# A decoder block on one core: two sets of one-hot and weight tiles, with other tensor work between the banks of the outer products

## What is computed

```python
xn = batch_norm(inputs)                        # over all 1792 tokens
q = (xn @ w_q.T)                               # 2 x 8 heads x 128
sim = einsum('pbnhd,hkpd->pbnhk', q, keys_p)   # 32 scores per half and head
scores, idx = top_k(sim, 8)                    # best 8 of 32, twice
sc, pk = top_k(scores[0][:, None] + scores[1][None, :], 8)
indices = expert numbers of these 8 pairs      # idx[0] * 32 + idx[1]
hmid = sigmoid(sc) * gelu(inputs . down[indices])
out = sum over heads and picks of hmid * up[indices]
```

## Time and profile before

| | us |
|---|---|
| three runs | 558.0, 559.16, 560.76 |
| median | 559.16 |
| the profiled execution | 559.34 |
| its span, from the first to the last instruction | 557.5 |
| TensorE busy | 436.3 (78%) |
| VectorE busy | 426.0 (76%) |
| ScalarE busy | 216.6 (39%) |
| GpSimd busy | 157.7 (28%) |

### The profile page before, as it was taken

The page is one execution under the profiler, slowest core; times in us unless marked ns, Lnnn a source line. Parts: engine busy times, 40 slices in busy tenths (PEclk is TensorE's granted clock), DMA queues, the critical chain, the costliest instruction groups (busy, mean ns, idle before and its releaser), DMA issues. The chain is left out here.

```text
span 557.5 us, 14244 instructions
## 1 busy us (share of the span) xinstructions
PE 436.3 (78%) x5223; PEld 342.7 (61%) x5223; DVE 426.0 (76%) x1693; ACT 216.6 (39%) x401; POOL 157.7 (28%) x205
## 2 busy tenths in 40 slices
PE   2899999989999999999985366738668386664757
PEld 1677777665868778787674145637456274563747
DVE  2999999866555545555457999997999979999582
ACT  1555545566544545445455032142331423213130
POOL 1433333700000000000000541736617366173610
PEclk9999999999999999999989575755857658677596
DMA  9991000200575564653000000000000000000000
GB/s 220 220 208 37 0 0 0 77 2 2 119 192 133 156 175 116 194 130 110 4 1 0 1 1 3 11 0 5 11 2 10 0 2 9 2 11 1 3 9 12
DMA packets 8730, 30.51 MB, mean 55 GB/s; under 512 B 696, under 2 KB 4280, under 8 KB 8408
## 3 DMA queue, kind: packets, MB, share of 16 engines
q1 hardware_dynamic: 8680, 29.89, 21.4%
HBM read 28.97 MB, written 0.92 MB: 54 GB/s over the span
## 5 line engine op out<-in xcount | busy, mean ns | idle before, releaser
L1272 PE MATMUL PS<-b_hi,AR 128*128 128x16 f16 x896 | 48.8, 174 | 38.4 <-DVEq L934 38.4
L1272 PEld LDWEIGHTS PS<-b_hi,AR 128*128 128x128 f16 x896 | 48.1, 104 | 43.1 <-DVEq L934 43.1
L1242 PE MATMUL PS<-xlT,KB 128*128 (+1 forms) x112 | 36.7, 484 | 30.2 <-ACT AR L592 25.3
L1242 PEld LDWEIGHTS PS<-xlT,KB 128*128 128x128 f32 x112 | 25.3, 237 | 41.6 <-ACT AR L592 28.1
L341 POOL TENSOR_TENSOR xn<-xn,cexp 128x1280 f16<-128x1280 f16 x14 | 45.3, 3234 | 17.5 <-DVE xn L905 17.5
L1273 PE MATMUL PS<-b_lo,AR 128*128 128x16 f16 x896 | 48.6, 174 | 0.0
L1273 PEld LDWEIGHTS PS<-b_lo,AR 128*128 128x128 f16 x896 | 48.2, 104 | 0.0
L1068 PE MATMUL PS<-KA,AR 125*128 125x125 f32 x384 | 46.8, 272 | 0.8 <-ACT AR L415 0.8
L1152 PE MATMUL PS<-AR 125*64 125x128 f32 x768 | 46.5, 278 | 0.0
L780 DVE COPY AR<-PS 125x512 f32<-125x512 f32 x16 | 11.1, 692 | 44.3 <-PE PS L1142 44.3
L1134 PE MATMUL PS<-AR 128*64 128x500 f32 x192 | 43.8, 591 | 1.3 <-ACT XA L497 0.9
(11 more groups left out here) (145 smaller groups left out, 1035.2 us busy)
## 6 DMA issues: line engine op xcount, KB each, us to landing
AR<-ctx SPq DMA_DIRECT2D x16, 1344.0 KB
AR<-ctx SPq DMA_DIRECT2D x16, 156.0 KB
KB<-pack_b SPq DMA_DIRECT2D x1, 1280.0 KB, 13.2
XA<-pack_q SPq DMA_DIRECT2D x1, 1024.0 KB, 4.7
KA<-pack_a SPq DMA_DIRECT2D x1, 965.0 KB, 7.1
XA<-x SPq DMA_DIRECT2D x4, 224.0 KB
out<-res SPq DMA_DIRECT2D x7, 128.0 KB, 1.8
XA<-zeros SPq DMA_DIRECT2D x2, 64.0 KB
```

Source lines behind the costliest of these rows:

```text
L1242: last = mm(bank(6 + r % 2, k * 256, k * 256 + 256), wb("down")[:, v * U:(v + 1) * U], xlT[:, bass.ds(i * 2 * TILE, 2 * TILE)], **one)
L1272: mm(o, pick_u[:, n, :], b_hi[:, n, :], start=True, stop=False)
```

## The change

`pick_u`, `b_hi` and `b_lo` become pairs, used in turn by `slot`; the second lies in memory that the cross-attention has done with, and GpSimd clears its weight tiles after the last product of that stage. `gelu` shrinks to two duos. With that, `picks(i)` may run while `spread(i-1)` still reads: it waits for the end of `spread(i-2)` (`mix_psum` starts at 2) and for `first_u(i-1)`.

TensorE's order becomes `hidden(i)`, bank 0 of the spread, `gather(i-1)`, bank 1, `weight_transpose(i+1)` and `expert_transposes(i+1)`, bank 2, `key_scores(i+2, 0)` and `key_scores(i+2, 1)`, bank 3. ScalarE runs `gelus(i)` straight after `mix_copies(i-1)`, and the copies and `first_u` of duo i+1 at the end of duo i. GpSimd runs `experts(i+1, 0)`, `mix(i-1)`, `experts(i+1, 1)`, `residual(i)`. VectorE's order is the same.

```diff
-        gelu = take(V * TOK).rearrange("p (v n) -> p v n", v=V)
-        pick_u = take(U * TILE // 2).bitcast(F16).rearrange("p (n u) -> p n u", u=U)
+        gelu = take(V * 4 * TILE).rearrange("p (v s n) -> p v s n", v=V, s=2)
+        pick_u = [take(U * TILE // 2).bitcast(F16).rearrange("p (n u) -> p n u", u=U) for _ in range(2)]
+        late_hi = take(V * TILE).bitcast(F16).rearrange("p (n w) -> p n w", n=TILE)
+        late_lo = take(V * TILE).bitcast(F16).rearrange("p (n w) -> p n w", n=TILE)
...
-        b_hi = sb("b_hi", [128, TILE, 2 * V], F16)
-        b_lo = sb("b_lo", [128, TILE, 2 * V], F16)
+        b_hi = [sb("b_hi", [128, TILE, 2 * V], F16)[:, :, :], late_hi]
+        b_lo = [sb("b_lo", [128, TILE, 2 * V], F16)[:, :, :], late_lo]
         act_w = x2[:, :, :].rearrange("p a c -> p (a c)").rearrange("p (t v n) -> p t v n", t=2, v=V)
...
+            def mix(i, slot):
                 pool.wait_ge(s["mix_copied"], i + 1)
                 pool.wait_ge(s["h_done"], (V // 2) * (i + 1))
                 pool.sem_inc(s["apart_pool"], 1)
                 for t in range(2):
-                    nc.gpsimd.tensor_tensor(act_w[:, t], act_w[:, t], gelu[:, :, bass.ds(i * 2 * TILE + t * TILE, TILE)], ALU.mult).then_inc(s["mixed"], 1)
-
+                    nc.gpsimd.tensor_tensor(act_w[:, t], act_w[:, t], gelu[:, :, slot, t * TILE:(t + 1) * TILE], ALU.mult).then_inc(s["mixed"], 1)
+
+            pool.wait_ge(s["o2_psum"], PAIRS)
+            ch.did(nc.gpsimd.memset(b_hi[1], 0.0))
+            ch.did(nc.gpsimd.memset(b_lo[1], 0.0))
+            ch.wait()
+            pool.sem_inc(s["iota_done"], 1)
             pool.wait_ge(s["t_copied"], 8)
             residual(0)
...
-                mix(i - 1)
+            def duo(i, slot, ahead=True):
                 if ahead:
                     experts(i + 1, 0)
+                mix(i - 1, 1 - slot)
+                if ahead:
+                    experts(i + 1, 1)
                 pool.wait_ge(s["out_psum"], i)
                 pool.sem_inc(s["apart_pool"], 1)
                 residual(i)
-                if ahead:
-                    experts(i + 1, 1)
             with pool.Fori(0, (DUOS - 3) // 2) as i:
                 ch.enter(i, 24)
                 for j in range(2):
...
             def mix_copies(i):
-                act.wait_ge(s["mix_psum"], i + 2)
+                act.wait_ge(s["mix_psum"], i + 3)
...
 
-            def gelus(i):
+            def gelus(i, slot):
                 for r in range(V // 2):
                     act.wait_ge(s["h_psum"], (V // 2) * i + (r + 1))
-                    nc.scalar.activation(gelu[:, 2 * r:2 * r + 2, bass.ds(i * 2 * TILE, 2 * TILE)],
+                    nc.scalar.activation(gelu[:, 2 * r:2 * r + 2, slot, :],
                                          bank(6 + r % 2).rearrange("p (v n) -> p v n", v=2), ACT.Gelu).then_inc(s["h_done"], 1)
...
-                nc.scalar.activation(pick_u[:, :, 0:V], eu8[:, :, :], ACT.Relu, scale=-1.0, bias=1.0).then_inc(s["first_u"], 1)
-
-            def duo(i):
+                nc.scalar.activation(pick_u[slot][:, :, 0:V], eu8[:, :, :], ACT.Relu, scale=-1.0, bias=1.0).then_inc(s["first_u"], 1)
+
+            def duo(i, slot):
                 if after(i, 1):
                     mix_copies(i - 1)
+                gelus(i, slot)
                 if before(i, 2):
                     normed(i + 2, 0)
-                expert_copies(i)
-                if before(i, 1):
-                    weights(i + 1, 0)
+                    normed(i + 2, 1)
                 if after(i, 1):
                     rows(i - 1)
-                first_u(i)
-                gelus(i)
-                if before(i, 2):
-                    normed(i + 2, 1)
                 if before(i, 1):
                     weights(i + 1, 1)
+                    expert_copies(i + 1)
+                if before(i, 2):
+                    weights(i + 2, 0)
+                if before(i, 1):
+                    first_u(i + 1, 1 - slot)
             for n in range(2):
                 for t in range(2):
                     normed(n, t)
             for t in range(2):
                 weights(0, t)
-            duo(0)
+            expert_copies(0)
+            weights(1, 0)
+            first_u(0, 0)
+            duo(0, 0)
             with act.Fori(0, (DUOS - 3) // 2) as i:
                 for j in range(2):
-                    duo(2 * i + (1 + j))
-            duo(DUOS - 2)
-            duo(DUOS - 1)
+                    duo(2 * i + (1 + j), (1 + j) % 2)
+            duo(DUOS - 2, (DUOS - 2) % 2)
+            duo(DUOS - 1, (DUOS - 1) % 2)
             rows(DUOS - 1)
...
 
-            def picks(i):
+            def picks(i, slot):
                 dve.wait_ge(s["mix_psum"], i + 1)
+                dve.wait_ge(s["first_u"], i + 1)
...
             dve.wait_ge(s["h_done"], (V // 2) * DUOS)
+            dve.wait_ge(s["out_psum"], DUOS - 1)
             for b in range(4):
                 dve.wait_ge(s["bank_spread"], b + 1)
...
-            pe.sem_inc(s["mix_psum"], 1)
+            pe.sem_inc(s["mix_psum"], 2)
             pe.sem_inc(s["sim_psum"], 2)
...
                         pe.wait_ge(s["ew_read"], i + 1)
                     elif r == 1:
-                        pe.wait_ge(s["res_ready"], i + 1)
+                        if after(i, 1):
+                            pe.wait_ge(s["res_ready"], i)
                     else:
                         pe.wait_ge(s["h_done"], (V // 2) * i + (r - 1))
...
 
-            def spread(i, by_bank=False):
-
-                pe.wait_ge(s["picks"], i + 1)
-                pe.wait_ge(s["first_u"], i + 1)
-                if after(i, 1):
-                    pe.wait_ge(s["mix_copied"], i)
-                for n in range(TILE):
-                    o = bank(n // 32, (n % 32) * 16, (n % 32) * 16 + 16)
-                    mm(o, pick_u[:, n, :], b_hi[:, n, :], start=True, stop=False)
-                    last = mm(o, pick_u[:, n, :], b_lo[:, n, :], start=False, stop=True)
-                    if by_bank and n % 32 == 31:
-                        last.then_inc(s["bank_spread"], 1)
-                if not by_bank:
+            def spread(i, slot, b, by_bank=False):
+
+                if b == 0:
+                    pe.wait_ge(s["picks"], i + 1)
+                    pe.wait_ge(s["first_u"], i + 2)
+                    if after(i, 1):
+                        pe.wait_ge(s["mix_copied"], i)
+                for n in range(32 * b, 32 * b + 32):
+                    o = bank(b, (n % 32) * 16, (n % 32) * 16 + 16)
+                    mm(o, pick_u[slot][:, n, :], b_hi[slot][:, n, :], start=True, stop=False)
+                    last = mm(o, pick_u[slot][:, n, :], b_lo[slot][:, n, :], start=False, stop=True)
+                if by_bank:
+                    last.then_inc(s["bank_spread"], 1)
+                elif b == 3:
                     last.then_inc(s["mix_psum"], 1)
 
-            def gather(i):
+            def gather(i, shown):
                 pe.wait_ge(s["x2s_ready"], i + 1)
-                pe.wait_ge(s["h_done"], (V // 2) * (i + 1))
+                pe.wait_ge(s["h_done"], (V // 2) * shown)
                 pe.wait_ge(s["res_ready"], i + 1)
                 for t in range(2):
...
-            def duo(i):
-                weight_transpose(i)
+            def duo(i, slot):
+                by_bank = not before(i, 1)
+                hidden(i)
+                spread(i, slot, 0, by_bank)
+                if after(i, 1):
+                    gather(i - 1, i + 1)
+                spread(i, slot, 1, by_bank)
                 if before(i, 1):
-                    key_scores(i + 1, 1)
-                expert_transposes(i)
-                if after(i, 1):
-                    gather(i - 1)
+                    weight_transpose(i + 1)
+                    expert_transposes(i + 1)
+                spread(i, slot, 2, by_bank)
                 if before(i, 2):
                     key_scores(i + 2, 0)
-                hidden(i)
-                spread(i, by_bank=not before(i, 1))
+                    key_scores(i + 2, 1)
+                spread(i, slot, 3, by_bank)
             key_scores(0, 0)
             key_scores(0, 1)
             key_scores(1, 0)
-            duo(0)
+            key_scores(1, 1)
+            weight_transpose(0)
+            expert_transposes(0)
+            duo(0, 0)
             with pe.Fori(0, (DUOS - 3) // 2) as i:
                 for j in range(2):
-                    duo(2 * i + (1 + j))
-            duo(DUOS - 2)
-            duo(DUOS - 1)
-            gather(DUOS - 1)
+                    duo(2 * i + (1 + j), (1 + j) % 2)
+            duo(DUOS - 2, (DUOS - 2) % 2)
```

More of the change, by code:

```diff
@@ L306, in _ @@
                     rotate(2 * i + j, j)
-            ch.did(nc.gpsimd.memset(b_hi[:, :, :], 0.0))
-            ch.did(nc.gpsimd.memset(b_lo[:, :, :], 0.0))
+            ch.did(nc.gpsimd.memset(b_hi[0], 0.0))
+            ch.did(nc.gpsimd.memset(b_lo[0], 0.0))
```

(46 more changed lines are left out.)

9 lines of the change are left out of this document (4 added, 5 removed).

## The result

The changed kernel took 603.28 us in the median (602.48 to 604.43, four runs), the kernel before 559.96 on the same chip: ratio 1.0779 [1.0741, 1.0817]. The profiled execution took 603.41 us, its span 601.6. The forecast was 613 in a range of 581 to 628, so it held, and 10 us of its 54 need an account. The answers to the earlier trace rows first: the page's engine line, then the stretches cut at spread starts (stretch, length, busy time of TensorE, its loads, VectorE, ScalarE and GpSimd, then the granted clock).

What follows compares the result with a forecast made beforehand. VectorE was taken to set the pace, in periods of 34.7 us. First period +9.4, four more +35.2, T(5) to T(6) +3.3 and the end +6.2 sum to +54 us, so 613 us from 559.2; range 581 to 628.

Steps and rivals of the forecast that it cites:

- T(0): Start of spread(0), T(i) being the start of spread(i), in the last stage: stays at 340.0 us.
- First period: T(0) to T(1), with no gather and the half clock: 44.0 us against 34.64, +9.4.
- From T(5) to T(6): Period without key scores, its picks meeting the mix: 31.4 us against 28.17, +3.3.
- Second set of tiles: Removes the wait of picks(i) for spread(i-1), which never ended last: worth 0.
- Hidden and gelus covered: Behind the mix copies, ready 13.2 us after L912; spread comes at 15.7 or later, 2.5 us to spare.
- K: First key score in TensorE's new order, which VectorE must await: ready at T+16.2 us, ends 15.7 and 18.1.
- The mix: GpSimd's weight product, now in the midst of VectorE's L929 and L932: costs VectorE 4.65 us a period.
- the end: gather(5) inside spread(6): last gather ends at T(6)+19.2 us against T+13.05, +6.2, ends +4 and +11.
- B: Mix slips past VectorE in whole or half, 6 times up to 4.65 us less: 585 to 600 us; chance 0.22.
- C: TensorE later still if the clock stays low, K = 18.1: 626 us; chance 0.08.
- D: VectorE not held up for key scores, period 30.75, mix escapes it too: 550 us; chance 0.04.
- E: Shorter chain (scores at full clock, gather 4.7 us) and half the mix: 590 to 600 us; chance 0.06.

Runs made afterwards that it cites:

- experiment 3: Changed kernel with one set of tiles again, picks(i) waiting for the end of spread(i-1): 606.38 us, 1.0815 of the kernel before.
- experiment 4: Changed kernel with GpSimd's weight product multiplying only one of its eight slices: 581.05 us, 1.0355 of the kernel before.
- 10: Changed kernel with gather(5) ahead of bank 0 of the last spread, in the last step alone: 600.92 us, 1.0716 of the kernel before.
- experiment 12: 7 with VectorE's loop written out and the product's second half held until VectorE's candidate sums have ended: 543.36 us, 0.9689 of the kernel before.
- experiment 1: Changed kernel with key_scores(i+2, 0) moved to behind bank 0 of the spread: 574.76 us, 1.0259 of the kernel before.
- 11: The kernel before with VectorE's loop over the duos written out: 560.71 us, 1.0007 of the kernel before.
- 7: Changed kernel: half 0 scores behind bank 0, gather behind bank 1 (last step: ahead of bank 0), mix after its step's picks, half 1 weights before row copy: 553.58 us, 0.9874.
- experiment 9: 7 with VectorE's loop written out and the product's second half held until VectorE has issued its candidate sums: 551.59 us, 0.983 of the kernel before.

## Why the prediction came out as it did

**What held, with small errors.** T(0) at 340.86 for the 340.04 of before (forecast: unmoved). First period 43.69 for the 44.0 forecast, VectorE starting half 0 at T+16.9 for T+16.8. From the start of half 0 to L923 6.84 for 6.85. From T(5) to T(6) 30.25 for 31.4. Place and kind of both costs: the wait ahead of half 0 on the key score, and the L941 beside the mix. Second set of tiles 0: nearly (1.8 us in the last step, experiment 3). Hidden and gelus covered: yes, no spread started on them. The added clears cost nothing that shows, within the 0.8 at T(0).

**The step that was mis-sized: K, the first key score, T+16.2.** VectorE started half 0 at T+14.8 (399.33 - 384.55) where the forecast had 16.3. TensorE was on time up to the transposes (forecast: from T+10.65; measured: 395.23, T+10.7). I took the 20 transposes from the earlier trace rows, 2.31 us, a row at half the clock; they took 1.28. The stretches around them show it (bank 0 with the gather's start, and from there to the middle of half 0's ranking):

```profile
384.55:391.20 6.65, 6.65 (x87) 6.65 (x88) 6.26 (x72) 0.00 (x0) 1.32 (x6) 0.50 0.00 0
391.20:404.85 13.65, 9.70 (x232) 8.44 (x231) 6.63 (x66) 2.37 (x5) 3.57 (x7) 1.00 0.05 14
```

The clock is at 0.50 (1.2 GHz) up to 391.20, inside the gather, and at 1.00 (2.4 GHz) from there on; the transposes had been moved behind the gather, so into the fast stretch. That is 1.03 us; the score, 0.98 at that clock where I took 1.5, is the rest. The earlier trace rows already had 0.90 in the window of a gather and 0.50 in that of a lone spread: the rows for the fast price were there, and I priced by the place from which the instruction came, not by the one to which it went. The Trainium skill, "TensorE: Matmul & The Clock Gate", "HAM oscillation", has the clock fall where TensorE idles. With that the trace agrees: ahead of this spread TensorE has nothing to do from 376.9 on, and the clock is at 1.00 from 377.5 to about 381 and at 0.50 from there to the spread's start; 7.65 us of that time is the wait for the picks. It then stays at 0.50 through 1.7 us of outer products and 4.9 us of gather without a gap.

```profile
384.55 0.17 PE L1287 MATMUL PS<-AR 128*128 128x16 f16 x1 [7.65 <-DVEq L946]
```

**The mix, 4.65 a period.** Measured 4.1: the four L941 took 10.89 us from the first start (409.80) to the last end (420.69), for 6.8 with L343 alone ahead of them (3.17 by the earlier trace rows and three of 1.22 by the earlier trace rows), and the cut of experiment 4 gave back 3.8 of it. Right in place, 12% too dear. With K it makes 2.0 us a period, 8 us in the four, of the 10 that the whole was off. The other 2: T(5) to T(6) came out 1.1 under (L923 0.7 earlier, the mix 0.45 cheaper), and the end took 18.25 for 19.2. There the terms written down add up to 19.4; the last gather began at T(6)+12.3 (592.87) for their 14.2, with no wait for VectorE's last product, and took 5.9 for 5.2, so two misses partly cancel.

**Rivals.** B (the mix slips past) fell: it hits in each of the six picks. C (TensorE later still) fell by the clock; in one period of experiments 3 and 10 it did come true, for 1.2 us. D (VectorE not held up) fell here, but its period of 30.75 is the one that experiment 12 reached, once scores and mix were put right: 30.7. E, the short chain with half the mix, had the score's clock right; its gather of 4.7 took 6.45 (386.25 to 392.70), and the mix cost 4.1, not half.

**Where 43 us went.** By the experiments, which are ratios and so independent of one trace: 29 us for the key scores' place (1); the product, by experiment 4, is 24 us in the changed kernel, but most of it was lost before as well, on L884 or, in every second period, covered by the jump (11). What experiment 1 leaves is 14.5 us by its ratio. Its trace has some 6 of them after T(6), where 10 gets back up to 5.2, and 7 before: two periods that hold the product and the jump together (37.2 and 37.5 us for 34.8), and the last, 30.0 for 28.2, where the product now meets the picks.

## What to carry to other kernels

Before moving work on an engine, write down for each consumer what it comes to next and when, and price every producer's new place against that time: here one key score moved past two banks, a gather and the transposes cost 29 us, and the second set of tiles that came with it gave back some 2. When instructions of two engines hold each other up (here VectorE's with two inputs against GpSimd's products), put the other engine's work beside stretches of another kind by an explicit event, and raise that event when the work has ended, not when it is issued. A null in the time is no null in the trace: removing the jump of the loop gave nothing only because it had covered a collision of the same size.

## What was unexpected of the hardware

**VectorE and GpSimd in turns.** Beside back-to-back L941, neither engine blocked the other for good: the records one by one have L941 starting at 412.90, 414.13 and 417.32, and L355 from 412.99 to 416.32 and 416.27 to 419.61. GpSimd's own two products stretched from 2.36 to 3.33 us each, VectorE's from 1.22 to 3.3, so the pair cost VectorE 4.1 us and GpSimd 1.9. L343 is passed over altogether for L934 when it comes behind L932 (4.37 us for 2.40), as L341 was in the earlier trace rows; why the one is passed over and the other takes turns is open. The Trainium skill, "SBUF — State Buffer", "Who interferes with whom", says that the first to issue has the shared pair for the whole instruction. The trace agrees that an instruction, once it runs, isn't interrupted (L941 of 414.13 ends 1.1 us after the product's first half, at 416.32). It doesn't agree on who is first: L343 starts at 407.52 and L934 at 408.43, and it is L934 that takes its 1.22.

**What doesn't contend.** VectorE's maxima out of PSUM (1.67 us for 16) and its rankings out of SBUF (L914, 0.17 us each) kept their times beside L357 in experiment 12.

**Outer products don't feel the clock.** A bank of 64 matmuls of 16 columns took 1.70 us at the granted clock 0.50 (384.55 to 386.25) and 1.61 at 1.00 (396.35 to 397.96), while the 20 transposes of 128 columns went from 2.31 to 1.28. So the low clock in a spread is nearly free, and dear for whatever stands behind it.

**A loop's jump leaves VectorE idle for 2.6 to 2.9 us** where nothing covers it (experiments 1, 7 and 11). **Its semaphores run ahead of its work:** an increment with no wait ahead of it was seen by GpSimd at 406.23, 0.4 us before the sums issued ahead of it began at 406.65 (experiment 9).
